# Swapped head copies, moved values and scale, split loads of x, and line loops that read and write other layouts, in an eight-stage kernel on one core

## The chip, the core and the metric

One core of a Trainium2 chip runs the whole program. The metric is the device time of one execution in microseconds. The engines are TensorE (PE; PEld is its weight load), VectorE (DVE), ScalarE (ACT), GpSimd (POOL) and SyncE (SP, which only issues transfers).

## What is computed

Eight images of 64 channels, 32x32, pass through a non-local block (attention over all 1,024 positions of an image), four recurrent passes of a nine-tap convolution (down, up, right, left), and then four token stages (window attention, spectral mixing, linear attention, experts), which the change does not touch. The first two, cut to what matters:

```python
def _L0_conv_ref(x, w_theta, w_phi, w_g, w_last):
    xf = x.reshape(B, C, H * W)
    theta = einsum('kc,bcn->bkn', w_theta, xf)          # 32 x 1024 an image
    phi, g = ...                                        # likewise
    attn = softmax(einsum('bkn,bkm->bnm', theta, phi), axis=-1)
    y = einsum('bnm,bkm->bkn', attn, g)
    return einsum('ck,bkn->bcn', w_last, y).reshape(B, C, H, W) + x

def _pass_fwd(out, w, b, axis):                         # _pass_bwd: the same from the last line back
    def step(carry, x):
        new = x + relu(conv1d(carry, w, b))
        return new, new
    ...
# forward and backward over rows (axis 2), then forward and backward over columns (axis 3)
```

## The kernel before

`setup_stage` loads x (two transfers of 1 MB, one on the queue of SyncE, one on that of ScalarE) and four small weights, zeroes some tiles on GpSimd and VectorE and writes the identity. Its block ends only when x has landed (`sp.wait_ge(x_in, 32)`).

`nonlocal_stage` is one block. Images are taken in two quads of four (q); image im of a quad has its 32 channels of theta and phi on partitions 32 im to 32 im + 31, which is also its row tile in TensorE. `project` makes theta and phi of a quad (L177), ScalarE and VectorE copy them to SBUF (L283, L312). Then `score(q, k, pair)` (L193) makes, for two images, the 128x1024 block of scores of 128 positions: two halves of 512 columns, each from the row tile of its image, into PSUM tile `ps[im]`. VectorE takes the maximum of each block (L316), ScalarE its exponential with the sum beside it (L289); the result is thrown away, only maximum and sum are kept. There are 64 such blocks of 128 rows, 16 groups of four. `score` of a pair waits until the exponentials of the same pair in the group before are done. Behind the last block come `values` (L202: g for all images, from x), the logarithm of the sums, the cut of maximum minus logarithm into three bf16 pieces (L318 to L326), `turn_shift` (L209: those pieces turned so that positions lie along the free axis) and copies of both to SBUF.

Then the attention: 32 units u (quad, half of the positions, block k). `score_t(u)` makes the transposed scores of four images with four products on four row tiles (L225) and adds the shift with four bf16 products of 3 rows (L229); ScalarE exponentiates them pair by pair (L302) through a ring of three PSUM tiles; `attend(u)` multiplies with the values (L241). TensorE's order is attend(u), score_t(u+2), and behind the first two units of each group of eight one `output` (L250) for the group before. VectorE copies the heads (L337) and adds the outputs to `m.rows` (L341).

`weights_stage` prepares weights. `conv_passes` runs 61 steps over the lines of a grid: TensorE adds the line by the identity (L385) and five shifted products (L388), VectorE adds bias, takes the maximum and so makes the new line (L405), ScalarE saves it to the grid (L419) and fetches the line two steps ahead into `added` (L414). TensorE waits for `fetch_ok` and, ahead of the shifted products, for `line_ok`. It runs first on `m.rows`, then `rows_to_cols_stage` (L449) copies everything into `m.cols`, it runs on `m.cols`, and `cols_to_tokens_stage` (L468) copies into `m.x`, where the token stages read. Both moves are three copies of 64x2048 on VectorE and one on ScalarE. GpSimd works out the spectral weights beside the vertical passes.

## Time and profile before

| | us |
|---|---|
| three timed runs | 1627.47, 1628.1, 1633.12 (median 1628.1) |
| the profiled run | 1628.84, its span 1627.1 |
| PE busy | 1440.0 (89% of the span) |
| DVE busy | 680.8 (42%) |
| ACT busy | 563.2 (35%) |
| POOL busy | 137.8 (8%) |
| mean granted TensorE clock | 0.919 |

The share of busy time is a mean over stages with different limits. A TensorE record is one pass; an fp32 product has two, with a load of weights for each. Times of the trace count from the first instruction. The clock is told as a share of 2.4 GHz, 0.5 being 1.2 GHz; for the first 23 us of this span there is no record of it, and the length of a pass tells it.

### The profile page before, as it was taken

What the parts mean: (1) busy time and instruction counts of PE and PEld (TensorE: products, weight loads), DVE (VectorE), ACT (ScalarE), POOL (GpSimd) and SP (SyncE); (2) the same over time, 40 slices, a digit from 0 to 9 for tenths busy, and PEclk for the clock granted to TensorE, in tenths of its full rate; (3) what the DMA queues carried; (4) which work ended last, traced back from release to release, by engine and by line L of the source; (5) the groups of instructions that cost most, each with busy time, mean ns of one, the idle gap of its engine ahead of it and who ended that gap; (6) DMA issues with size and microseconds to landing.
All of it is one profiled execution on the core that took longest, in us unless ns stands there. A gap on an engine that the chain in (4) does not pass through costs nothing. (4 is left out here: it accounts for less than half of the span.)

```text
span 1627.1 us, 25795 instructions
## 1 busy us (share of the span) xinstructions
PE 1440.0 (89%) x9714; PEld 977.4 (60%) x9714; DVE 680.8 (42%) x963; ACT 563.2 (35%) x913; POOL 137.8 (8%) x243
## 2 busy tenths in 40 slices
PE   4888997887887799999988999999999999958767
PEld 1335225776776699999985555555555555537544
DVE  3664013113112677777753333332333323326562
ACT  2654674223223443434343222222222212214250
POOL 5000002930000111111100000000000000003000
PEclk9555897999998999999999999999999999979977
DMA  4900000000000500000000000000000000040001
GB/s 98 104 1 1 1 1 3 0 0 0 0 0 21 186 0 0 0 0 0 0 1 1 0 0 0 0 0 0 0 0 0 0 0 0 0 100 5 1 1 52
DMA packets 34241, 23.48 MB, mean 14 GB/s; under 512 B 24621, under 2 KB 28749, under 8 KB 34205
## 3 DMA queue, kind: packets, MB, share of 16 engines
q1 hardware_dynamic: 33837, 21.92, 6.2%
q10 hardware_dynamic: 368, 1.07, 0.3%
q8 instruction: 24, 0.39, 0.1%
q14 instruction: 12, 0.10, 0.0%
HBM read 20.80 MB, written 2.18 MB: 14 GB/s over the span
## 5 line engine op out<-in xcount | busy, mean ns | idle before, releaser
L948 PE MATMUL sp_f<-hankel,sp_ut 128*128 x2304 | 420.9, 344 | 0.0
L948 PEld LDWEIGHTS sp_f<-hankel,sp_ut 128*128 128x128 f16 x2304 | 222.8, 98 | 216.7 <-issue 27.5
L987 ACT COPY sp_sums<-sp_f 64x1023 f32<-64x1023 f32 x128 | 129.0, 1008 | 427.6 <-PE sp_f L948 427.6
L1010 DVE COPY sp_sums<-sp_f 64x1024 f32<-64x1024 f32 x128 | 155.2, 1212 | 91.9 <-PE sp_f L948 91.9
L1008 DVE COPY sp_mix<-mix 128x512 f32 x64 | 27.3, 427 | 281.6 <-PE sp_f L948 281.6
L959 PE MATMUL sp_o<-sp_sums,sp_mix 128*64 128x128 f32 (+2 forms) x1024 | 123.7, 392 | 0.0
L193 PE MATMUL nl_ps<-mix 32*128 32x512 f32 x256 | 94.2, 1065 | 22.0 <-ACT nl_spent L289 22.0
L388 PE MATMUL convh<-runningh,toeplitz 128*128 128x128 f32 x610 | 85.9, 287 | 15.2 <-DVE runningh L405 15.2
L388 PE MATMUL convv<-runningv,toeplitz 128*128 128x128 f32 x610 | 85.8, 287 | 15.2 <-DVE runningv L405 15.2
L316 DVE TENSOR_REDUCE nl_max<-nl_ps 128x1 f32<-128x1024 f32 x64 | 74.0, 1218 | 43.3 <-PE nl_ps L193 43.3
L388 PEld LDWEIGHTS convh<-runningh,toeplitz 128*128 128x128 f32 x610 | 74.4, 192 | 26.7 <-DVE runningh L405 26.7
L388 PEld LDWEIGHTS convv<-runningv,toeplitz 128*128 128x128 f32 x610 | 74.2, 191 | 26.7 <-DVE runningv L405 26.7
L289 ACT ACTIVATE nl_spent<-nl_ps,nl_max 128x1024 bf16<-128x1024 f32 x64 | 71.3, 1114 | 46.7 <-DVE nl_max L316 46.7
L959 PEld LDWEIGHTS sp_o<-sp_sums,sp_mix 128*64 128x64 f32 x1024 | 63.2, 134 | 37.4 <-issue 15.6
L193 PEld LDWEIGHTS nl_ps<-mix 32*128 32x128 f32 x256 | 36.8, 310 | 78.6 <-ACT nl_spent L289 44.8
L302 ACT ACTIVATE nl_probs_t<-nl_ps 128x1024 f32<-128x1024 f32 x64 | 62.0, 1021 | 25.6 <-PE nl_ps L229 25.6
L688 PEld LDWEIGHTS s_ps<-win_x,queries 128*128 128x128 f32 x512 | 68.4, 194 | 2.6
L688 PE MATMUL s_ps<-win_x,queries 128*128 128x128 f32 x512 | 68.5, 277 | 0.0
L705 PE MATMUL z_ps<-win_heads_t,win_vo 128*128 128x128 f32 x512 | 62.6, 275 | 2.2 <-ACT win_heads_t L767 2.2
L717 PE MATMUL z_ps<-win_probs_t,win_xt 128*128 128x128 f32 x512 | 62.6, 275 | 1.4 <-ACT win_probs_t L761 0.8
L761 ACT ACTIVATE win_probs_t<-t_ps 128x512 f32<-128x512 f32 x32 | 19.1, 598 | 123.5 <-PE t_ps L699 123.5
L705 PEld LDWEIGHTS z_ps<-win_heads_t,win_vo 128*128 128x128 f32 x512 | 59.7, 192 | 2.6 <-ACT win_heads_t L767 2.6
(299 smaller groups left out, 1828.4 us busy)
## 6 DMA issues: line engine op xcount, KB each, us to landing
hankel<-phi_rows SPq DMA_DIRECT2D x32, 256.0 KB, 6.0
ex_w<-in_L_ffn_weight SPq DMA_DIRECT2D x1, 2080.0 KB
m_plus<-in_L_ffn_M_phi_plus SPq DMA_DIRECT2D x2, 1024.0 KB, 14.0
m_minus<-in_L_ffn_M_phi_minus SPq DMA_DIRECT2D x2, 1024.0 KB, 16.3
out<-x SPq DMA_DIRECT2D x8, 256.0 KB, 3.3
x<-in_x SPq DMA_DIRECT2D x1, 1024.0 KB, 8.5
x<-in_x ACTq DMA_DIRECT2D x1, 1024.0 KB, 12.4
ar<-in_L_ffn_M_u SPq DMA_DIRECT2D x2, 192.0 KB, 3.1
```

The source lines that it names most:

```text
L193: mm = nc.tensor.matmul(ps[im][:, c * BANK:(c + 1) * BANK], theta[q][rows_of(im), k * P:(k + 1) * P], phi[q][rows_of(im), c * BANK:(c + 1) ...
L289: nc.scalar.activation(spent[im][:, :], ps[im][:, :], ACT.Exp, bias=nmax[:, q, k, im:im + 1], accum_out=rsum[:, q, k, im:im + 1]).then_inc ...
L302: nc.scalar.activation(probs_t[u % 2][:, 2 * pair:2 * pair + 2, :].rearrange("p a n -> p (a n)"), ps[j % 3][:, :], ACT.Exp).then_inc(p_ok, 1)
L316: nc.vector.tensor_reduce(nmax[:, q, k, im:im + 1], ps[im][:, :], axis=AX.X, op=ALU.max, negate=True).then_inc(mx_ok, 1)
L388: mm = nc.tensor.matmul(conv[odd][:, :, :], m.toeplitz[:, wn, s, :], running[1 - odd][:, :, s:s + PAIRS], start=False, stop=(s == SHIFTS - 1))
L688: mm = nc.tensor.matmul(s_ps[:, hg, w, :], queries[:, w, 4 * hg:4 * hg + 4, :].rearrange("p h n -> p (h n)"), m.win_x[:, w, :, :].rearrang ...
L705: mm = nc.tensor.matmul(o_ps, m.win_vo[:, h, :], heads_t[:, h // 4, :, (h % 4) * WINDOW:(h % 4 + 1) * WINDOW], start=(h == 0), stop=(h == ...
L717: mm = nc.tensor.matmul(z_ps[:, hg, w, :], xt[odd][:, w, :], probs_t[:, hg, w, :], start=True, stop=True)
L948: mm = nc.tensor.matmul(f_ps[b][:, lo:(half + 1) * BANK], ut[:, hu, b, i, :, :].rearrange("p a c -> p (a c)"), m.hankel[:, hf, ds(j * 2 + ...
L959: mm = nc.tensor.matmul(out_of(lo, cnt, par), mixk[n][:, SCALES - 1 - seg, par, :], sums[n][:, :, lo + par:lo + cnt:2], start=False, stop= ...
L987: nc.scalar.copy(sums[n][HALF[1], b, 1:T], f_ps[b][HALF[1], 0:T - 1]).then_inc(f_act, 1)
L1010: nc.vector.tensor_copy(sums[n][HALF[0], b, :], f_ps[b][HALF[0], :]).then_inc(f_dve, 1)
```

## The change

Setup: x comes in halves of two image pairs each, behind the small weights, on the same two queues, with a semaphore for each half (`m.x_in[q]`), and the block no longer waits for them. TensorE makes 24 products of the identity with itself there. The zeroing of `rows` moves into the non-local block, that of the `lin_` tiles to VectorE, that of `cols` goes.

Non-local: theta (whole) and phi (its second half of the columns) get copies with the two halves of the partitions swapped (`theta_b`, `phi_b`). Of a block of scores the first 512 columns come from the image's own row tile, the other 512 from the tile two further on, so that a pair of images fills all four. The four PSUM tiles are two pairs used in turn. `values` stands behind the first pair of scores. The shift is the negated maximum alone, with no logarithm, cut and turned by quads, the first quad's in the middle of the scores, the second's turned at units 2 and 6 of the attention. The reciprocals of the sums are spread over 32 channels, turned (`turn_scale`, once in each group of eight units) and multiplied onto the heads. In `score_t` the shifts of the first pair come ahead of the scores and those of the second behind them.

Lines: `conv_passes` is given an object that fetches and stores. The horizontal passes read their lines out of `m.rows` on the way forward (two copies of 64x128 a line), keep them in `m.cols`, fetch them from there on the way back and store each line straight into `m.x` (four copies of 64x64). Line 0 and the last line are brought to `m.x` by GpSimd. The two moving stages are gone.

```diff
@@ setup_stage
+    WARM = 24
...
+                for q in range(2):
+                    eng.dma_start(m.x[HALF[p], 2 * q:2 * q + 2, :], ins["x"][4 * q + p:4 * q + 4:2].rearrange("g c h w -> c g (h w)")).then_inc(m.x_in[q], 16)
-                sp.wait_ge(x_in, 32)
+            @block.tensor
+            def _(pe):
+                pe.wait_ge(ident_ok, 1)
+                for n in range(WARM):
+                    mm = nc.tensor.matmul(warm_ps[:, :], m.ident[:, :], m.ident[:, :], start=True, stop=True)
+                mm.then_inc(warm, 1)
@@ nonlocal_stage, GpSimd
+                pool.wait_ge(q_act, 3)
+                pool.wait_ge(q_dve, 5)
+                for g in range(2):
+                    nc.gpsimd.tensor_copy(theta_b[HALF[1 - g], 1, :], theta[1][HALF[g], :]).then_inc(q_pool, 1)
...
+                    nc.gpsimd.tensor_copy(phi_b[HALF[1 - g], 1, :], phi[1][HALF[g], BANK:T]).then_inc(q_pool, 1)
...
+                nc.gpsimd.memset(m.rows[:, :, :, :], 0.0).then_inc(zeroed, 1)
+        TURN_AT = {2: 0, 6: 1}
+        SCALE_AT = 4
@@ TensorE
+                def score(s):
+                    q, k, pair = s // (2 * NB), s // 2 % NB, s % 2
...
+                    elif s == 1:
+                        pe.wait_ge(ex_ok, 2)
+                    elif s == 2:
+                        pe.wait_ge(v_c, 2)
                     else:
+                        pe.wait_ge(ex_ok, 2 * (s - 1))
+                    if s == PAIRED // 2:
+                        pe.wait_ge(q_pool, 4)
+                    for j, im in enumerate((2 * pair, 2 * pair + 1)):
+                        nc.tensor.matmul(slots(s)[j][:, 0:BANK], theta[q][rows_of(im), k * P:(k + 1) * P], phi[q][rows_of(im), 0:BANK], start=True, stop=True)
+                    for j, im in enumerate((2 * pair, 2 * pair + 1)):
+                        far = rows_of((im + 2) % QUAD)
+                        nc.tensor.matmul(slots(s)[j][:, BANK:T], theta_b[far, q, k * P:(k + 1) * P], phi_b[far, q, :], start=True, stop=True).then_inc(s_ok, 1)
...
+                    shifted(0, True)
...
+                        pe.wait_ge(p_ok, 2 * u - 1)
                     for im in range(QUAD):
+                        mm = nc.tensor.matmul(out[im], phi[q][rows_of(im), k * P:(k + 1) * P], theta[q][rows_of(im), c * BANK:(c + 1) * BANK],
+                                              start=(im >= 2), stop=(im < 2))
+                        if im == 1:
                             mm.then_inc(t_ok, 1)
+                    shifted(1, False).then_inc(t_ok, 1)
...
+                def turn_scale(w):
+                    q, c = w // NH, w % NH
+                    pe.wait_ge(wide_ok, q + 1)
+                    use_out()
+                    for k in range(NB // NH):
+                        mm = nc.tensor.matmul(o_ps[:, k * P:(k + 1) * P], wide[:, q, c * NB // NH + k, :, :].rearrange("p i c -> p (i c)"), m.ident[:, :],
+                                              start=True, stop=True)
+                    mm.then_inc(o_ok, 1)
...
+                score(0)
+                values()
+                for s in range(1, PAIRED):
+                    score(s)
+                pe.wait_ge(cut_ok, 1)
+                pe.wait_ge(ex_ok, ROWS - 2)
+                turn_shift(0, 0, ps[3][:, 0:BANK])
+                turn_shift(0, 1, ps[3][:, BANK:T]).then_inc(turn_ok, 1)
...
+                    if u in TURN_AT:
+                        pe.wait_ge(cut_ok, 2)
+                        use_out()
+                        turn_shift(1, TURN_AT[u], o_ps).then_inc(o_ok, 1)
+                    if u % NB == SCALE_AT:
+                        turn_scale(u // NB)
@@ ScalarE
-                nc.scalar.activation(rest[:, :, :, :], rsum[:, :, :, :], ACT.Ln).then_inc(ln_ok, 1)
@@ VectorE
+                    if n == ROWS // NQ + 1:
+                        dve.wait_ge(mx_ok, ROWS // NQ)
+                        cut(0)
...
+                nc.vector.tensor_copy(shift_t[0][:, :], ps[3][:, :]).then_inc(turn_c, 1)
+                dve.wait_ge(mx_ok, ROWS)
+                cut(1)
...
+                    nc.vector.tensor_tensor(heads[w % 2][:, :], y_ps, scale_t[w % 2][:, :], ALU.mult).then_inc(y_c, 1)
@@ lines
+class ColumnLines:
...
+    def column(self, pair, par, hp):
+        return self.rows[HALF[par], hp::2, :, ds(PADP + pair, 1)].rearrange("c r b a -> c b (r a)")
+
+    def token(self, pair, par, hp, p):
+        x = self.x[HALF[p], :, :].rearrange("c g (r a w) -> c g r a w", a=2, w=W)
+        return x[:, :, :, hp, ds(pair * 2 + par, 1)].rearrange("c g r w -> c g (r w)")
+
+    def fetch(self, copy, dst, pair, par):
+        for hp in range(2):
+            last = copy(dst[HALF[hp], :, :], self.column(pair, par, hp))
+        return last
...
+    def store(self, copy, line, pair, par):
+        for hp in range(2):
+            for p in range(2):
+                last = copy(self.token(pair, par, hp, p), line[HALF[hp], p::2, :])
+        return last
@@ hybrid_program
-            conv_passes(nc, m, m.rows, 0, "v", lambda block: spectral_mixing(nc, m, block, mixing_step))
-            rows_to_cols_stage(nc, m)
-            conv_passes(nc, m, m.cols, 2, "h")
-            cols_to_tokens_stage(nc, m)
+            vertical_passes(nc, m, mixing_step)
+            horizontal_passes(nc, m)
```

## Rows read from the trace of the kernel before

**Rows 1.** Windows: stretch, its length, each engine's busy time (records), clock, DMA.
```profile
27.95:146.66 118.71, 94.19 (x259) 36.83 (x257) 75.18 (x65) 72.56 (x127) 1.06 (x1) 0.52 0.34 42
146.66:165.96 19.30, 18.13 (x92) 16.09 (x92) 3.90 (x7) 5.92 (x7) 0.00 (x0) 0.50 0.00 1
165.96:258.34 92.38, 85.12 (x692) 22.73 (x692) 8.31 (x12) 62.01 (x64) 0.00 (x1) 0.96 0.00 1
...
394.85:400.92 6.07, 0.00 (x0) 0.00 (x0) 5.68 (x3) 3.71 (x1) 0.00 (x0) 0.81 0.00 0
...
517.58:524.32 6.74, 0.00 (x0) 0.00 (x0) 5.65 (x3) 3.68 (x1) 0.00 (x0) 0.54 0.00 0
```
**Rows 2.** Timeline of one group of scores, of 16: start, length, instruction.
```profile
93.30 6.05 PE L193 MATMUL nl_ps<-mix 32*128 32x512 f32 x16 [1.41 <-ACT nl_spent L289]
...
97.11 4.62 DVE L316 TENSOR_REDUCE nl_max<-nl_ps 128x1 f32<-128x1024 f32 x4 [2.84 <-PE nl_ps L193]
...
98.37 1.11 ACT L289 ACTIVATE nl_spent<-nl_ps,nl_max 128x1024 bf16<-128x1024 f32 x1 [2.86 <-DVE nl_max L316]
...
100.75 0.50 PEld L193 LDWEIGHTS nl_ps<-mix 32*128 32x128 f32 x4 [2.98 <-ACT nl_spent L289]
```
**Rows 3.** Groups by line: the projections up to 22.9 us, and from 23.7 us.
```profile
L177 PE MATMUL nl_ps<-x,nl_proj 128*64 128x512 f32 x10 | 4.5, 1068 | 3.8 <-ACT nl_last L280 3.8
...
L177 PE MATMUL nl_ps<-x,nl_proj 128*64 128x512 f32 x22 | 4.9, 596 | 0.0
```
**Rows 4.** Timeline of the setup and the start of the non-local stage.
```profile
1.39 0.29 POOL L78 TENSOR_SCALAR_AFFINE_SELECT ident<-ident 128x128 f32<-128x128 f32 x1 [0.23 <-POOL average L76]
...
13.96 0.26 POOL L150 MEMSET nl_proj<- 128x192 f32 x1 [7.03 <-POOLq L55]
...
16.48 0.54 DVE L309 COPY nl_proj<-nl_ps 64x96 f32<-64x96 f32 x2 [9.01 <-POOL nl_pieces L153]
...
18.78 9.24 PE L177 MATMUL nl_ps<-x,nl_proj 128*64 128x512 f32 x32 [3.81 <-ACT nl_last L280]
```
**Rows 5.** Timeline by engine between the last scores and the first probability.
```profile
146.66 13.92 PE L202 MATMUL nl_ps<-nl_proj,x 128*128 128x64 f32 x64 [2.55 <-ACT nl_spent L289]
...
161.46 1.23 DVE L328 CAST nl_shift_t<-nl_ps 128x1024 bf16<-128x1024 f32 x1 [10.45 <-PE nl_ps L209]
...
165.96 1.94 ACT L302 ACTIVATE nl_probs_t<-nl_ps 128x1024 f32<-128x1024 f32 x2 [1.34 <-PE nl_ps L229]
```
**Rows 6.** Timeline of the attention: a unit with an output, and a plain one.
```profile
214.73 1.13 PE L250 MATMUL nl_ps<-nl_heads,nl_last 128*64 128x256 f32 x8
...
215.78 1.07 PE L241 MATMUL nl_ps<-nl_probs_t,mix 128*32 128x512 f32 x8
...
216.78 1.14 PE L225 MATMUL nl_ps<-mix 32*128 32x512 f32 x8
...
218.07 1.13 PE L250 MATMUL nl_ps<-nl_heads,nl_last 128*64 128x256 f32 x8
...
227.50 1.14 PE L225 MATMUL nl_ps<-mix 32*128 32x512 f32 x8
...
229.96 1.14 PE L225 MATMUL nl_ps<-mix 32*128 32x512 f32 x8
```
**Rows 7.** Timeline of one conv step, of 61; the window of the horizontal loop's start.
```profile
295.38 1.39 PE L388 MATMUL convv<-runningv,toeplitz 128*128 128x128 f32 x10 [0.29 <-DVE runningv L405]
295.46 0.30 ACT L419 COPY rows<-runningv 128x128 f32 x1 [1.40 <-DVE runningv L405]
295.67 0.30 ACT L414 COPY addedv<-rows 128x128 f32 x1
...
296.61 0.39 PE L385 MATMUL convv<-addedv,ident 128*128 128x128 f32 x2
...
297.21 1.20 PEld L388 LDWEIGHTS convv<-runningv,toeplitz 128*128 128x128 f32 x10 [0.41 <-DVE runningv L405]
...
400.92:405.50 4.58, 4.21 (x18) 3.92 (x19) 0.96 (x4) 1.01 (x4) 0.00 (x0) 0.51 0.00 0
```

More of the change, by code:

```diff
@@ L198, in values @@
-                def values(half):
-                    pe.wait_ge(ex_ok, ROWS - 1 + half)
-                    for g in (2 * half, 2 * half + 1):
-                        for k in range(NB):
-                            mm = nc.tensor.matmul(ps[2 + half][:, (g % 2) * BANK + k * C:(g % 2) * BANK + (k + 1) * C], m.x[:, g, k * P:(k + 1) * P],
-                                                  proj[:, 2, :, :].rearrange("p a k -> p (a k)"), start=True, stop=True)
-                    mm.then_inc(v_ok, 1)
@@ L411, in _, with fetch, step @@
                 act.sem_inc(saved, 1)
-                def fetch(line, odd):
-                    nc.scalar.copy(added[odd][:, :, :], at(line)).then_inc(fetch_ok, 1)
-                def step(n, odd, line, ahead=None):
+                def fetch(pair, odd, back):
+                    (lines.refetch if back else lines.fetch)(nc.scalar.copy, added[odd][:, :, :], pair, odd).then_inc(fetch_ok, 1)
+                def step(n, odd, pair, back):
                     act.wait_ge(line_ok, n + 1)
-                    nc.scalar.copy(at(line), running[odd][:, :, PADP:PADP + PAIRS]).then_inc(saved, 1)
-                    if isinstance(ahead, int) and ahead >= 2 * TOP - 3:
-                        act.wait_ge(saved, n + 1)
-                    if ahead is not None:
-                        fetch(ahead, odd)
+                    (lines.store if back else lines.keep)(nc.scalar.copy, inner(running[odd]), pair, odd).then_inc(saved, 1)
@@ L463, in cols_to_tokens_stage @@
[L463 to L479 removed]
+                    step(n, n % 2, (2 * FWD - n) // 2, True)
@@ new lines, in vertical_passes, with horizontal_passes, ends, _ @@
+def vertical_passes(nc, m, mixing_step):
+    conv_passes(nc, m, RowLines(m), 0, "v", lambda block, saved, n: spectral_mixing(nc, m, block, mixing_step))
+def horizontal_passes(nc, m):
+    lines = ColumnLines(m)
+    def ends(block, saved, n):
+        @block.gpsimd
+        def _(pool):
+            for hp in range(2):
+                for p in range(2):
+                    src = m.rows[HALF[0], hp::2, p::2, PADP:PADP + 1].rearrange("c r g a -> c g (r a)")
+                    nc.gpsimd.tensor_copy(lines.token(0, 0, hp, p), src)
+            pool.wait_ge(saved, n)
+            lines.store(nc.gpsimd.tensor_copy, lines.at(W // 2 - 1, 1), W // 2 - 1, 1)
+    conv_passes(nc, m, lines, 2, "h", ends)
```

355 lines of the change are left out of this document (202 added, 153 removed).

## The prediction

> **What bounds the kernel now.** I first cut the span into stretches by the table of windows [rows 1]: 118.7 us of scores, 19.3 us between them and the first probability, 92.4 us of attention, and two stretches of 6.07 and 6.74 us in which TensorE does nothing. The change touches these, the 28 us ahead of them and the two line loops around the moves; the 1,100 us behind 524.3 us it leaves alone. Then I read who waits for whom in each.
>
> The scores go in groups of four rows of blocks, 16 groups, 7.45 us each (LDWEIGHTS at 93.30 and 100.75) [rows 2]. No engine is full: the four reductions take 4.62 us, the exponentials about the same. It is a ring: TensorE writes the first pair's two PSUM tiles (93.30 to 97.11, 3.81 us), VectorE reduces one (1.26 us), ScalarE exponentiates two (98.37 to 100.75, 2.38 us), and only then may TensorE write again. The 3.81 us are four passes of 0.86 us one after another, two products side by side. 0.86 us is the length of a 512-column pass at 1.2 GHz: in the projections such a pair took 0.86 us (10 records in 4.5 us) and then 0.43 us (22 records in 4.9 us) once the clock had risen to 2.4 GHz [rows 3]; the granted clock of the score stretch is 0.52 [rows 1].
>
> The attention is bound by TensorE's own sequence and a ring of about the same length: 2.46 us for a plain unit (227.50 to 229.96), 3.34 us for a unit with an output (214.73 to 218.07), of which output 1.05, attend 1.00, scores and shifts 1.29 [rows 6].
>
> A conv step is a ring of TensorE and VectorE, with ScalarE beside: it saves a line at 295.46, fetches at 295.67 and is done at 295.97; the product that needs the fetched line starts at 296.61, the next step's weight loads at 297.21, 1.83 us behind the last ones [rows 7].
>
> **Part 1, start.** The wait for x at the end of the setup goes; in its place stand 24 products of 128x128 fp32 from 1.68 us on, when the identity is written [rows 4]. A pass of 128 columns is 0.11 us at 2.4 GHz (10 records in 1.39 us, less the tail of the last [rows 7]), so 0.22 at 1.2, and a product two passes. All cold 10.6 us, all warm 5.3; I take 11 cold and 13 warm, 7.8 us, so the stage ends at 9.5 us, bound by these products, and the next begins at about 10.1 instead of 13.96 [rows 4]. From there to the turned weights in SBUF is GpSimd's four memsets and two copies, 13.96 to 17.02: 3.1 us, unchanged. The first projection no longer waits for the ScalarE copies, so it starts at 13.3 instead of 18.78. x had landed by 13.96 with both megabytes; its first half, now two small loads later, should be in by 12. I expect TensorE, idle for most of 9.5 to 13.3, to be back at 1.2 GHz, and the projections to take their 9.24 us again [rows 4]: they end at 22.5 instead of 28.0. If the clock holds they take 32 x 0.215 = 6.9 us, 2.3 less.
>
> **Part 2, values moved.** Their 64 records took 13.9 us at 1.2 GHz, between scores and attention [rows 5]. Now they stand behind the first score pair, right behind the projections, where the clock is up: 64 x 0.11 = 7.0 us, all on the path, since every later score is queued behind them. The end for a clock that falls first is 13.9. They wait for phi of the second quad, a copy of 1.2 us like the one at 161.46 (together about 1.35 us behind the last projection, the first score pair and VectorE's swapped copies lying in it). 22.5 + 1.35 + 7.0 + 1.15 for the next pair: VectorE's regular work starts at 32.0. GpSimd's swapped copies for the second quad, its memset and its placing of x run beside this; they are due at the seventeenth pair and at the first addition.
>
> **Part 3, scores.** Both halves of a row's columns go to four row tiles at once: two passes instead of four, so 3.81 - 2 x 0.86 = 2.1 us at 1.2 GHz and about 1.17 at 2.4 (the attention's eight records on four tiles take 1.14 [rows 6]). The four PSUM tiles are now two pairs with a ring each. The ring is 2.1 + 1.26 + 2.38 = 5.75 us for four rows (4.8 warm); the engines' floor is VectorE's 4.62 [rows 2]. Which clock? Before, at 1.2 GHz, the engine was busy 94 of 119 us on half its rows and never rose [rows 1]. Now it would be busy a third less of the time on all rows, about the same work in a little less time. I take 1.2 GHz. 30 pairs x 2.88 = 86.3 us from 32.0, plus 0.7 for the first quad's cut, which now stands in VectorE's queue between two reductions: the last pair's reductions start at 119.0.
>
> **Part 4, from scores to attention.** Gone are the logarithm, two table loads and one cut from the path. What is late next is VectorE: last reductions until 121.4, the shift's copy 1.2, then shifts and scores of the first unit, 2.3 us cold. First probability at 125.0 instead of 165.96 [rows 5]: 41.0 us earlier.
>
> **Part 5, attention.** It lasted 92.1 us from 165.96 (the window's 92.38 less the end of the block) [rows 1]. Added to TensorE's sequence: four turns of the sums (eight passes of 0.11 and a drain, nearest row the output's 1.05): 4.2 us; two half turns of the second shift in bf16, 0.45 each: 0.9. The multiplication takes the place of a copy of the same shape. The shifts are split: those of the first pair ahead of the scores, those of the second behind. A bf16 pass of 512 columns is half an fp32 pass of 0.43, 0.21 us. If tiles run free of one another the unit stays at 2.29 us of TensorE work (1.00 + 1.29) and the ring shrinks to 1.02 (an exponential) + 0.06 + 1.17 = 2.25: 0.17 less for 23 plain units, -3.9. If products start strictly in the order written, the second pair's scores stand behind the first pair's, which wait for their shifts: 2.29 + 0.21 = 2.50, +1 in plain units and +0.21 in the six with an output, +1.3. So between +1.2 and +7.4 in all. In the rows no product is seen overtaking another, so I take +7.4.
> The Trainium skill ("TensorE: Matmul & The Clock Gate", Part 3, What overlaps and what doesn't) says that products start and end strictly in program order whatever their tiles. By it the sum is +7.4; with free tiles it would be +1.2.
>
> **Part 6, lines.** Both moving stages go: 6.07 us, and of the second stretch the same 6.07, while 0.67 of it is the next stage's start [rows 1]. Added: the first fetch is four half copies instead of two (+0.4), the last save four quarter copies (+0.6). In the loop ScalarE has a save and two half fetches forward, four quarter stores and a fetch backward. A 128-element copy follows the next after 0.21 us [rows 7]; the strided move took 3.71 us for 2,048 elements [rows 1], 1.8 ns each, so 64 cost 0.09 + 0.12 = 0.2. Backward: 4 x 0.2 + 0.3 = 1.1 us from 295.46, to 296.56, against 296.61, and a wait would hurt only 0.39 us ahead of 297.21, from 296.82 on [rows 7]. Hidden, if a store costs under 0.26; at 0.3 it would cost 30 x 0.15 = 4.5 us. Line 0 and the last column go over GpSimd, beside. TensorE's pause shrinks from 7 to 2 us at one place and from 8 to 2.5 at the other: the loop's start took 4.58 us for 18 records at clock 0.51 [rows 7], some 1.6 more than warm. I take 1.3 for it and 0.5 for the norm (0 to 3).
>
> **Sum.** -41.0 + 7.4 - 12.1 + 1.0 - 1.8 = -46.5 us against a span of 1627.1, in a run of 1628.84, which is 0.7 above the median: 1628.1 - 46.5 = 1581.6.
>
> **Rivals.**
> A, free tiles in the attention: 6.2 less, 1575.4. The rows don't exclude it.
> B, the scores run at 2.4 GHz, and emptying PSUM decides: 30 pairs x 2.31 to 2.4 us is 14 to 17 us less, a warm start of the attention 2 more: 1564. For it: the values before it are warm and all row tiles are used; against: pauses of over 1 us in every 2.4. The Trainium skill ("TensorEngine Tiling (Array Packing)", PSUM Bottleneck) warns that after a fourfold speed-up the copy out of PSUM may be the limit. By that rule the group takes 4.62 us and not 5.75, which is this rival.
> C, values at 1.2 GHz: +6.9 us, 1588.5. For it: a pause before them; against: the projections just before are full work.
> D, the four products don't run side by side (it doesn't do what it says): the ring stays 7.45, +26 us, 1608. Against: the attention's scores, four tiles, eight records in 1.14 us [rows 6].
> E, slower than before: ScalarE's quarter copies with columns 256 bytes apart take over the backward loop. A store of 0.26 us is where it starts; at 0.66 a step takes 1.55 us more, 30 steps 46.5 us, the whole gain; above 0.66 the kernel is slower, at 0.8 it takes 1581.6 + 30 x 2.14 = 1646. Against: 1.8 ns an element in the strided move.
>
> **Chances.** Forecast 45% (1574 to 1589 by its own bounds), A 27, B 10, C 9, other prices of the conv loop and the start, 1585 to 1600, 4, D 2, E 3. The range takes all but the outer ends of B, D and E: 1564 to 1592. A measurement of this kernel tells about 0.5% (8 us) from no change. Faster by more: 95%; within 0.5%: 2%; slower: 3%.
>
> **What would show it.** First projection at 13.3 us; first warm pass of the values at 24 with 0.11 us between; groups of four rows 5.75 us apart (4.8: B; 7.45: D); first probability at 125; plain units 2.50 (2.29: A), units with an output 3.55; no pause over 2.5 us between the loops; conv steps still 1.83 to 1.90 us, backward too. The forecast is wrong if the score stretch runs at another clock or if the backward steps are longer.

## The result and the profile after

The changed kernel takes 1584.1 us (median of four runs, 1579.14 to 1585.12) against 1628.3 us for the kernel before (four runs beside it, 1627.47 to 1633.12): ratio 0.972, 95% interval 0.969 to 0.974. The forecast was 1581.6 us, its range 1564 to 1592. The profiled run took 1585.12 us, its span is 1583.3 us, 43.8 us less than before; the mean granted clock is 0.929 (before 0.919).

The windows of the changed kernel, cut where its stages change (stretch, length, busy time of PE, PEld, DVE, ACT, POOL with records, clock, DMA); the lines of before that they answer to are [rows 1]. The clock has no record before 6.7 us, so the 1.00 of the first line doesn't hold for all of it; the passes themselves tell: 22 of 0.21 us up to 6.6 us, which is 1.2 GHz, then 26 of 0.11 us:

```profile
0.00:9.98 9.98, 7.97 (x48) 7.78 (x48) 2.71 (x8) 0.00 (x0) 1.14 (x9) 1.00 0.71 147
9.98:21.81 11.83, 9.35 (x45) 2.99 (x45) 3.27 (x6) 5.17 (x8) 2.41 (x4) 0.86 0.65 145
21.81:30.55 8.74, 8.39 (x74) 7.53 (x72) 3.49 (x3) 3.35 (x5) 7.01 (x5) 1.00 0.27 53
30.55:118.56 88.01, 60.59 (x249) 15.16 (x249) 73.58 (x66) 69.92 (x120) 8.67 (x5) 0.56 0.45 52
118.56:123.33 4.77, 3.37 (x22) 1.82 (x22) 4.57 (x11) 2.33 (x4) 0.00 (x0) 0.50 0.00 0
123.33:220.19 96.86, 92.51 (x734) 30.49 (x730) 13.14 (x19) 62.07 (x64) 0.00 (x1) 0.92 0.00 1
220.19:240.20 20.01, 15.08 (x122) 13.04 (x122) 11.43 (x25) 10.70 (x14) 4.90 (x21) 0.50 0.04 6
357.35:478.20 120.85, 106.33 (x732) 91.14 (x732) 22.40 (x65) 78.54 (x243) 2.23 (x8) 0.98 0.00 0
478.20:1583.30 1105.10, 1019.64 (x7044) 709.39 (x7044) 522.66 (x712) 338.12 (x449) 54.23 (x151) 0.96 0.05 14
```

The first probability stands at 123.33 us where it stood at 165.96: 42.6 us are won up to there. The attention gives back 4.5 us (96.86 against 92.38). Between the vertical and the horizontal passes 6.1 us are gone; horizontal passes and second move together give 2.6 us (from 123.4 to 120.85). The vertical passes take 0.6 us more, and the token stages, whose code is the same, 2.3 us more. -42.6 + 4.5 - 6.1 - 2.6 + 0.6 + 2.3 = -43.9 us, the 43.8 us of the spans but for rounding.

The start, timeline of TensorE (start, length, instruction, idle before it and what ended that); before, the projections began at 18.78 [rows 4] and the values took 13.92 us [rows 5]:

```profile
1.73 7.97 PE L79 MATMUL warm_ps<-ident 128*128 128x128 f32 x48 [1.73 <-POOL ident L87]
...
13.10 1.60 PE L205 MATMUL nl_ps<-x,nl_proj 128*64 128x512 f32 x4 [2.44 <-DVE nl_proj L372]
...
23.30 7.33 PE L215 MATMUL nl_ps<-nl_proj,x 128*128 128x64 f32 x64 [0.35 <-DVE mix L381]
```

One turn of the score ring, timeline; it answers to [rows 2]:

```profile
88.49 2.36 DVE L407 TENSOR_REDUCE nl_max<-nl_ps 128x1 f32<-128x1024 f32 x2 [0.22 <-PE nl_ps L236]
...
89.56 1.22 PE L233 MATMUL nl_ps<-mix 32*128 32x512 f32 x2 [1.12 <-ACT nl_spent L358]
...
89.57 1.22 PE L236 MATMUL nl_ps<-nl_phi_b,nl_theta_b 32*128 32x512 f32 x2
...
89.75 1.11 ACT L358 ACTIVATE nl_spent<-nl_ps,nl_max 128x1024 bf16<-128x1024 f32 x1 [0.24 <-DVE nl_max L407]
...
90.58 1.06 PE L233 MATMUL nl_ps<-mix 32*128 32x512 f32 x2
...
90.88 1.11 ACT L358 ACTIVATE nl_spent<-nl_ps,nl_max 128x1024 bf16<-128x1024 f32 x1
91.70 2.36 DVE L407 TENSOR_REDUCE nl_max<-nl_ps 128x1 f32<-128x1024 f32 x2 [0.86 <-PE nl_ps L236]
...
92.14 0.29 PEld L233 LDWEIGHTS nl_ps<-mix 32*128 32x128 f32 x2 [2.06 <-ACT nl_spent L358]
...
94.28 1.23 DVE L407 TENSOR_REDUCE nl_max<-nl_ps 128x1 f32<-128x1024 f32 x1 [0.22 <-PE nl_ps L236]
```

The fp32 products of a pair take two passes one after another, 89.56 to 91.70 (2.14 us), where before there were four: the two halves of a row start 0.01 us apart. VectorE starts a pair at 88.49 and at 94.28: 5.79 us for four rows where it was 7.45. It still idles (0.22 and 0.86 us), because a pair's first product waits for both exponentials of that PSUM pair: the first ends 1.1 us before the second, and its tile stands empty. This turn ran at 1.2 GHz, like most of the stretch.

### The profile page after: what moved, and what is told of

Read it like the earlier page. It is cut to its first block and busy times, and to the rows that moved or that the text cites. A ratio compares the mean times of both kernels' runs of the same rounds, so it can differ in the third digit from the quotient of the medians.

```text
span 1583.3 us, 26273 instructions
## 1 busy us (share of the span) xinstructions
PE 1423.7 (90%) x9794; PEld 968.1 (61%) x9794; DVE 679.3 (43%) x977; ACT 601.3 (38%) x1029; POOL 138.5 (9%) x251
## 5 line engine op out<-in xcount | busy, mean ns | idle before, releaser
L1113 PEld LDWEIGHTS sp_o<-sp_sums,sp_mix 128*64 128x64 f32 x1024 | 63.1, 134 | 37.4 <-issue 15.5
L233 PE MATMUL nl_ps<-mix 32*128 32x512 f32 x128 | 61.3, 1052 | 26.2 <-ACT nl_spent L358 26.0
L365 ACT ACTIVATE cols<-nl_ps 128x1024 f32<-128x1024 f32 x64 | 62.1, 1022 | 29.6 <-PE nl_ps L269 29.6
L522 DVE SCALAR_TENSOR_TENSOR runningh<-convh,conv_bias,addedh 128x128 f32<-128x128 f32 x61 | 21.5, 352 | 96.1 <-PE convh L505 96.1
L948 DVE TENSOR_REDUCE win_max<-s_ps 128x16 f32<-128x1024 f32 x32 | 39.2, 1225 | 53.3 <-PE s_ps L842 53.3
```

What stands on the lines that cost most here:

```text
L233: nc.tensor.matmul(slots(s)[j][:, 0:BANK], theta[q][rows_of(im), k * P:(k + 1) * P], phi[q][rows_of(im), 0:BANK], start=True, stop=True)
L365: nc.scalar.activation(probs_t[u % 2][:, 2 * pair:2 * pair + 2, :].rearrange("p a n -> p (a n)"), ring[j % 3][:, :], ACT.Exp).then_inc(p_o ...
L1113: mm = nc.tensor.matmul(out_of(lo, cnt, par), mixk[n][:, SCALES - 1 - seg, par, :], sums[n][:, :, lo + par:lo + cnt:2], start=False, stop= ...
```

## Experiments

All edits are to the changed kernel, except where another is named. Where one time is given, the kernel was run once; it is compared with 1584.1 us, and its trace with the trace of the changed kernel. Four runs of the changed kernel lie 6 us apart, and beside own_tiles, values_back, stores_twice and one_pause the kernel before took 1631.4 us in the median, 3 us more than beside the changed kernel. So a single time says little below some 5 us, and the readings rest on the stages in the traces.

**Release by rows.** The products of a row wait for the exponential of that row's own PSUM tile, and a row's two halves are issued together.

```diff
-                    elif s == 1:
-                        pe.wait_ge(ex_ok, 2)
...
-                    else:
-                        pe.wait_ge(ex_ok, 2 * (s - 1))
...
                     for j, im in enumerate((2 * pair, 2 * pair + 1)):
+                        if s == 1 or s >= 3:
+                            pe.wait_ge(ex_ok, max(2 * (s - 2), 0) + j + 1)
                         nc.tensor.matmul(slots(s)[j][:, 0:BANK], ...)
-                    for j, im in enumerate((2 * pair, 2 * pair + 1)):
                         far = rows_of((im + 2) % QUAD)
                         nc.tensor.matmul(slots(s)[j][:, BANK:T], ...)
```

> The changed kernel with one thing moved: a row's two score products wait for the exponential of the row that last used their PSUM tile, not for both rows of the pair, and are issued row by row. Theory (the scores are bound by the ring of a pair: TensorE 2.1 us, a reduction 1.26, two exponentials and the way back 2.38, together 5.75 for four rows): a row's own ring is 2.1 + 1.26 + 1.13 + 0.15 = 4.65 for four rows, so VectorE's four reductions of 4.62 us become the bound, even at 1.2 GHz. The last pair's reductions then start some 17 us earlier (at 100 to 101 us instead of 117.4) and the run takes about 1567 us. Rival 1 (TensorE's 1.2 GHz is the bound as such): the group stays at 5.75 us and the time at 1584. Rival 2 (products of the next row wait until those of the row before have ended): the ring grows to 2.1 + 2.1 + 1.26 + 1.13 and the group to 6 us or more, 1588 or slower.

Measured: 1564.8 us (1563.16 to 1565.64, four runs), ratio 0.961 (0.958 to 0.963). The windows of its scores, and of the part of them that ran at 1.2 GHz:

```profile
31.80:101.19 69.39, 65.98 (x236) 20.74 (x232) 69.17 (x66) 68.14 (x120) 6.38 (x4) 0.85 0.54 63
35.60:45.80 10.20, 10.20 (x36) 4.26 (x36) 10.16 (x10) 10.12 (x19) 2.70 (x2) 0.50 0.92 119
```

VectorE is busy 69.17 of 69.39 us: it is the bound, 4.6 us for four rows. The granted clock of the stretch rose from 0.56 to 0.85, but the gain doesn't hang on it: from 35.6 to 45.8 us the clock was 0.50, and VectorE was busy 10.16 of 10.20 us. So at 1.2 GHz it was the wait for two exponentials, and not the length of the products, that held the ring at 5.8 us. The third and fourth units of the attention started 3.31 and 2.29 us behind the ones before instead of 4.55 and 3.26: both kernels began the attention at 1.2 GHz, but here the clock rose 5.0 us behind the first probability (at 110.7 us) and there 9.7 us behind it.

**The tiles of the own image again.** The second half of a row's columns from the row tile of its own image, once with release by pairs (own_tiles), once with release by rows (own_by_row).

```diff
-                        far = rows_of((im + 2) % QUAD)
-                        nc.tensor.matmul(slots(s)[j][:, BANK:T], theta_b[far, q, k * P:(k + 1) * P], phi_b[far, q, :], start=True, stop=True).then_inc(s_ok, 1)
+                        nc.tensor.matmul(slots(s)[j][:, BANK:T], theta[q][rows_of(im), k * P:(k + 1) * P], phi[q][rows_of(im), BANK:T], start=True, stop=True).then_inc(s_ok, 1)
```

> The changed kernel with one part undone: the second half of a row's columns comes again from the row tile of the row's own image (theta, phi), so that a pair of rows is four passes one after another; the swapped copies are still made and not read. My theory: the ring of four rows is 7.45 us as in the kernel before instead of 5.78, 15 groups, +25 us: 1609 us. Rival (the ring was shorter in the changed kernel because its four PSUM tiles are used as two pairs in turn, not because of the tiles): 1584 to 1590 us.

> Release row by row, and both halves of a row's columns again from the row tile of its own image (the swapped copies are still made, but not read), so that a row is four passes one after another. Theory 1 (what the swapped copies bought was only a shorter ring, and with release by rows the ring of each slot has room): at 2.4 GHz a slot's ring is 1.75 products + 1.2 reduction + 1.35 exponential = 4.3 us against VectorE's 4.6 us for four rows, so 1565 us as with the swapped copies. Theory 2 (the copies are needed because the clock is low in this stretch): at 1.2 GHz the ring is 3.45 + 2.55 = 6.0 us for four rows, 16 x 1.4 = 22 us more, 1587 us. The granted clock of the score stretch tells which.

Measured: own_tiles 1609.7 us (one run), own_by_row 1590.8 us (1589.96 to 1595.16, four runs), ratio 0.978 (0.976 to 0.980). In own_tiles the last reduction comes 110.92 us behind the fourth, 60 rows: 7.39 us for four rows, as before the change, against 85.62 us and 5.71. So the tiles gave the change's shorter ring; the turns of the PSUM tiles gave nothing. For own_by_row theory 2 held, 6.29 us for four rows. The window of its scores:

```profile
34.10:128.50 94.40, 93.25 (x236) 56.37 (x235) 72.82 (x66) 71.11 (x121) 5.13 (x3) 0.52 0.40 46
```

TensorE is busy 93.25 of 94.40 us, and its clock is 0.52 all the same. The busy time counts any row tile at work; each of them still waits. One PSUM tile's turn lasts 6.33 us (its products start at 71.76 and again at 78.09 us): 3.8 us for the row's four passes one after another, 1.26 for the reduction and 1.25 for the exponential. So the ring of a single tile sets the end, and the products at 1.2 GHz are its longest part. Over the 60 rows behind the fourth the swapped copies are worth 25.3 us with release by pairs (110.92 against 85.62) and 25.0 us with release by rows (94.38 against 69.39).

**Values behind the scores again.**

```diff
-                score(0)
-                values()
-                for s in range(1, PAIRED):
+                for s in range(PAIRED):
                     score(s)
-                pe.wait_ge(cut_ok, 1)
                 pe.wait_ge(ex_ok, ROWS - 2)
+                values()
+                pe.wait_ge(cut_ok, 1)
+                pe.wait_ge(v_c, 2)
```

(The two copies of the values move to the same place on ScalarE and VectorE, and the third pair of scores no longer waits for them but for theta and phi of the second quad.)

> The changed kernel with one part undone: the products of the values stand behind the last pair of scores again and not behind the first. My theory (their price is their clock): before the steady scores 8.5 us less (7.3 for the products, 1.2 for the copy), behind them 13.9 at 1.2 GHz and 1.2 for the copy, of which 1.2 to 3 us lie beside the last reductions and exponentials; +4 to +6 us, 1588 to 1590 us, first probability 4 to 6 us later than 123.3. Rival (the products are full work and bring the clock up wherever they stand): 7.3 us there too, and the attention starts at full clock: 1578 to 1583 us.

Measured: 1591.4 us, first probability at 135.19, 11.9 us later. Timeline of TensorE, and the window of the values:

```profile
115.17 13.91 PE L215 MATMUL nl_ps<-nl_proj,x 128*128 128x64 f32 x64 [1.13 <-ACT nl_spent L356]
```

```profile
115.00:129.40 14.40, 13.91 (x64) 13.72 (x64) 1.72 (x3) 3.47 (x7) 0.00 (x0) 0.50 0.00 0
```

The price was right (13.9 us at 1.2 GHz, no rise of the clock in full work), the gain at the front was not: steady work began 3.3 us earlier, not 8.5. The second pair uses the PSUM tiles of the first and waits for its exponentials until 26.41; in the changed kernel that wait lies beside the values. So the move is worth more at the first probability, 11.9 us, than the difference of two lengths. Of these the end shows 6.2: the attention's first to last probability took 1.1 us less, the stretch from there to the first line of the vertical passes 1.4, and the token stages 3.0, all of the same code as in the changed kernel.

**No warm products.** The TensorE block of the setup is left out.

> The changed kernel without the 24 warm products. Theory (they bind the end of the setup, at 9.7 us, and their warmth is lost before the projections): the non-local stage begins at 4 to 4.5 us instead of 9.98, the turned weights are there at 7.7, and the first projection starts when the first half of x has landed, 9.6 us instead of 13.1. The projections still begin at 1.2 GHz, the rest is 3.5 us earlier: 1580.5. Rival (the warm products bring the clock up for the projections or the values): without them the projections take 9.2 us or more instead of 8.7 and the values 13.9 us instead of 7.3, which takes back all of it: 1584 to 1588.

Measured: 1581.5 us; first projection at 9.42, released by x's arrival:

```profile
9.42 2.83 PE L199 MATMUL nl_ps<-x,nl_proj 128*64 128x512 f32 x6 [4.21 <-DMA x<-in_x]
```

First probability at 119.57 instead of 123.33. From the first to the last start of a projection it is 8.22 us, with the 24 products 8.19. They held up the next stage by 3.7 us, and nothing of it came back up to the first probability.

**Shifts behind the scores for all four images.**

```diff
-                    shifted(0, True)
...
-                                              start=(im >= 2), stop=(im < 2))
-                        if im == 1:
-                            mm.then_inc(t_ok, 1)
+                                              start=True, stop=False)
+                    shifted(0, False).then_inc(t_ok, 1)
                     shifted(1, False).then_inc(t_ok, 1)
```

> The changed kernel with all four shifts of an attention unit behind its scores, as before the change. Theory (row tiles run free of one another, so a shift ahead of one pair's scores hides under the other pair's, and the first probability of a unit may start before the last shifts): undoing it brings the ring back to 1.02 + 0.06 + 1.38, plain units back from 2.29-2.37 to 2.46 us, some 0.1 x 24 = 2 to 3 us longer attention (96.9 to about 99.5 us). Rival (products start strictly in the order written, and the split only costs): plain units fall to 2.29 us by TensorE's work or stay, the attention gets shorter by up to 5 us.

Measured: 1585.2 us. Plain units are 2.55 us apart (163.93 - 161.38 by the exponentials below) instead of 2.29 and 2.37 by turns; first to last probability 90.22 us instead of 88.30. In the kernel before they were 2.46 us apart with all shifts behind [rows 6]; what the other 0.09 us are, no run shows.

```profile
158.83 1.94 ACT L363 ACTIVATE cols<-nl_ps 128x1024 f32<-128x1024 f32 x2 [1.41 <-PE nl_ps L251]
161.38 1.94 ACT L363 ACTIVATE cols<-nl_ps 128x1024 f32<-128x1024 f32 x2 [0.61 <-PE nl_ps L251]
163.93 1.94 ACT L363 ACTIVATE cols<-nl_ps 128x1024 f32<-128x1024 f32 x2 [0.61 <-PE nl_ps L251]
```

The 1.9 us between the two sums hide a difference of the clock: here it rose 6.2 us behind the first probability and there 9.7, so the first three starts of a unit took 9.72 us against 11.01. In the 28 starts behind them, all at 2.4 GHz, it is 79.58 against 76.37 us: the split is worth 3.2 us.

**Fetch ahead of the stores** in the backward loop.

```diff
-                        step(k * 2 + odd, odd, k * (-1) + (FWD - odd), True)
+                        act.wait_ge(line_ok, k * 2 + odd + 1)
                         fetch(k * (-1) + (FWD - 1 - odd), odd, True)
+                        step(k * 2 + odd, odd, k * (-1) + (FWD - odd), True)
```

> The changed kernel with ScalarE's order on the way back of the horizontal passes turned round: it fetches the line two steps ahead first and then makes the four quarter stores of the new line. Theory (the backward step is 1.946 instead of 1.865 us because the fetch stands behind four stores of 0.31 us and TensorE waits for it): the fetch ends 0.3 us behind the new line instead of 1.55, the step falls back to 1.865 us, 30 steps give 2.4 us. Rival (the stores slow the step by themselves, through SBUF writes 256 bytes apart or VectorE's wait for the saved line): the step stays at 1.95 us. Time 1581 against 1584 by the theory, which a single time can't tell; the step in the trace does.

Measured: 1580.0 us. 30 backward steps took 56.00 us, as many forward ones 56.01; in the changed kernel 58.34 and 56.00. Timeline of ScalarE and VectorE in two backward steps, with the identity product in the first; first the changed kernel, then with the fetch first:

```profile
431.32 1.23 ACT L612 COPY x<-runningh 64x64 f32 x4 [0.54 <-DVE runningh L522]
432.57 0.30 ACT L604 COPY addedh<-cols 128x128 f32 x1
432.65 0.35 DVE L522 SCALAR_TENSOR_TENSOR runningh<-convh,conv_bias,addedh 128x128 f32<-128x128 f32 x1 [1.48 <-PE convh L505]
...
433.00 0.48 PE L502 MATMUL convh<-addedh,ident 128*128 128x128 f32 x2 [0.39 <-DVE runningh L522]
...
434.71 0.35 DVE L522 SCALAR_TENSOR_TENSOR runningh<-convh,conv_bias,addedh 128x128 f32<-128x128 f32 x1 [1.72 <-PE convh L505]
```

```profile
434.16 0.30 ACT L605 COPY addedh<-cols 128x128 f32 x1 [0.41 <-DVE runningh L522]
434.37 1.23 ACT L613 COPY x<-runningh 64x64 f32 x4
...
435.50 0.35 DVE L522 SCALAR_TENSOR_TENSOR runningh<-convh,conv_bias,addedh 128x128 f32<-128x128 f32 x1 [1.55 <-PE convh L505]
...
437.33 0.35 DVE L522 SCALAR_TENSOR_TENSOR runningh<-convh,conv_bias,addedh 128x128 f32<-128x128 f32 x1 [1.48 <-PE convh L505]
```

In the changed kernel the four stores take 1.23 us, the fetch ends at 432.87, and the identity product starts at 433.00 instead of running ahead of the line at 432.65: steps of 1.83 and 2.07 us by turns. With the fetch first 1.83 and 1.90.

**Stores twice.** Eight quarter copies a line in the backward loop, four of them into a spare tile of the same layout.

```diff
-    def store(self, copy, line, pair, par):
-        for hp in range(2):
-            for p in range(2):
-                last = copy(self.token(pair, par, hp, p), line[HALF[hp], p::2, :])
+    def store(self, copy, line, pair, par, into=(None,)):
+        for x in into:
+            for hp in range(2):
+                for p in range(2):
+                    last = copy(self.token(pair, par, hp, p, x), line[HALF[hp], p::2, :])
```

> The changed kernel with the four quarter copies of the backward horizontal loop issued twice, the first four into a spare tile of the same layout: eight copies of 0.31 us stand for four of 0.62. The law of my rival E, every store above 0.26 us lengthens a step by four times the excess: 1.87 + 4 x 0.36 = 3.3 us a step, 30 steps, +40 us against the changed kernel's 1.95: 1624 us. Rival, ScalarE's own work is the bound and nothing more: 8 x 0.31 + 0.30 for the fetch + 0.2 = 3.0 us a step, +31 us, 1615 us. Second rival, half of the excess because a fetch serves the step after the next: 2.6 us a step, +20 us, 1604 us.

Measured: 1608.0 us; the last 30 steps in 79.64 us against 58.34. The 28 of them that have the stores in the loop take 2.55 and 2.84 us by turns, 2.7 a step. Timeline of ScalarE in one step:

```profile
434.54 0.30 ACT L607 COPY addedh<-cols 128x128 f32 x1
434.75 1.23 ACT L616 COPY spare_xh<-runningh 64x64 f32 x4
...
436.00 1.23 ACT L616 COPY x<-runningh 64x64 f32 x4
...
437.25 0.30 ACT L607 COPY addedh<-cols 128x128 f32 x1
```

No idle time stands before any of them: ScalarE's own row of copies is the bound, 8 x 0.31 + 0.21 = 2.7 us from fetch to fetch (my sum of 3.0 counted 0.3 us too much around it). The second rival's 2.6 us lies near too, but it has ScalarE waiting, which it doesn't. Rival E's law was too steep by half: the steps cost 21.3 us more than with four stores, not 40. By an estimate from this row of copies, 4 x s + 0.21 us a step, a store would have to cost 0.8 us, not 0.66, before the loop ate the whole gain of 46.5 us (4 x 0.8 + 0.21 = 3.4, 1.55 more than 1.87).

**Three edits together**: release by rows, fetch first, and warm products where TensorE waits anyway (5 products in the setup, 11 behind the transposes of the small weights). The same without any warm products is lean.

```diff
-    WARM = 24
+    WARM = 5
...
                 mm.then_inc(lt_ok, 1)
+                for n in range(11):
+                    nc.tensor.matmul(ps[1][:, 0:P], m.ident[:, :], m.ident[:, :], start=True, stop=True)
                 pe.wait_ge(wt_c, 2)
```

> Three edits together: products of a row wait only for their own slot's last exponential; the backward line loop fetches ahead of its stores; of the 24 warm products 5 stay in the setup and 11 move behind the transposes of the small weights, beside the ScalarE and GpSimd copies that the first projection waits for. My theory (the three terms are independent: 1564.8 us with the first alone, -2.4 for the fetch, and at the start -3.65 for what the 24 products held up and up to -1.3 more because the projections now start at full clock, a pair 0.43 us apart from the first one): 1557.5 us. First projection at 9.5 us, last projection starting 6.8 us behind the first instead of 8.2. Rival, the projections wait for x and not for TensorE: they start again late or pause, 1559 to 1560. Rival, VectorE's 4.6 us per four rows is not the end and the earlier start only shifts the clock: back to 1562 or more.

> The same as the kernel with the three edits, but all 24 warm products left out and none moved. My theory, that warm products pay only where they stand beside a wait directly ahead of the projections: 1558.8 us, first projection at 9.4 us, last projection starting 8.2 us behind it. If the difference to the kernel with the moved products is 0 or below, they are worth nothing here.

Measured: three edits 1556.0 us (1553.95 to 1558.85, four runs), ratio 0.956 (0.954 to 0.959); lean 1559.5 us (1558.11 to 1559.67, four runs), ratio 0.959 (0.957 to 0.960). Timeline of TensorE with the three edits:

```profile
1.74 2.50 PE L79 MATMUL warm_ps<-ident 128*128 128x128 f32 x10 [1.74 <-POOL ident L87]
...
5.45 5.00 PE L197 MATMUL nl_ps<-ident 128*128 128x128 f32 x22
10.38 1.08 PE L207 MATMUL nl_ps<-x,nl_proj 128*64 128x512 f32 x4
```

All 22 passes ran at 1.2 GHz (5.00 us, 0.227 us each) and ended 0.9 us after x was there (9.53 in lean), and the projections right behind them ran at 2.4 GHz from the first one on (the granted clock rose at 10.3 us), 6.53 us from first to last start against 8.43 in lean. The last reduction is 0.85 us earlier than in lean. The medians are 3.5 us apart, but the intervals of the two ratios overlap and the two traces differ by 0.2 us in span, so more than 1 us for the moved products isn't shown.

**Pauses filled.** On top of the three edits, three products of 128x128 fp32 behind the last line step of both line blocks and three more ahead of the first horizontal step (filled); the same between the vertical and the horizontal passes alone (one_pause, whose diff this is).

```diff
                     mm.then_inc(conv_ok, 1)
+                def filler():
+                    for n in range(3):
+                        nc.tensor.matmul(conv[0][:, :, :], m.ident[:, :], m.ident[:, :], start=True, stop=True)
+                if tag == "h":
+                    filler()
                 steps(pe, step)
+                if tag == "v":
+                    filler()
```

> The kernel with the three edits, and in both line blocks three products of 128x128 fp32 behind the last line step (beside the last VectorE and ScalarE work), and in the horizontal block three more ahead of the first step (beside the first fetches). Theory (the clock falls behind these pauses because TensorE did nothing in them): full clock in the first 12 us of the horizontal passes and of the first layer norm, 1 to 2 us less than the kernel with the three edits. Rival (the clock falls for another reason, or these stretches are bound by other engines): within 0.5 us of it, or up to 0.5 us slower, as the three products end after the wait that they stand beside.

> The kernel with the three edits, and products to fill the pause between the vertical and the horizontal passes alone: three of 128x128 fp32 behind the last vertical step, three ahead of the first horizontal one. In the trace of the kernel that filled three pauses the first horizontal line was ready 3.59 us behind the last vertical one instead of 4.89. Theory, that 1.3 us is a gain: the same 3.6 us here, and 1.3 us less than the 1556.0 us of the three edits, 1554.7. Rival, the time is given back in the clock of later stretches: 1556 to 1558 us.

Measured: filled 1558.0 us (1556.52 to 1558.92, four runs), ratio 0.958 (0.956 to 0.959); one_pause 1558.6 us (1554.7 to 1559.4, five runs), ratio 0.955 (0.953 to 0.956), with runs of before between 1629.09 and 1635.07 us beside it, 4 us higher in the median than beside the others. Timeline of TensorE and VectorE of one_pause:

```profile
330.85 0.35 DVE L529 SCALAR_TENSOR_TENSOR runningv<-convv,conv_bias,addedv 128x128 f32<-128x128 f32 x1 [1.48 <-PE convv L504]
...
331.84 0.91 PE L510 MATMUL convh<-ident 128*128 128x128 f32 x6 [0.36 <-PEq L494]
...
333.11 1.28 PE L504 MATMUL convh<-runningh,toeplitz 128*128 128x128 f32 x10
...
334.43 0.35 DVE L529 SCALAR_TENSOR_TENSOR runningh<-convh,conv_bias,addedh 128x128 f32<-128x128 f32 x1 [1.54 <-PE convh L504]
```

From the last vertical to the first horizontal line it is 3.58 us (334.43 - 330.85), 3.59 in filled, and 4.90 with the three edits alone; the window of 334.4 to 345 us has clock 1.00 instead of 0.84 (filled against the three edits). So a filled pause gives 1.3 us in its place; the whole doesn't show it. In the traces the attention of filled took 0.8 us more and its token stages 1.7 more. The kernels with the three edits lie at 0.955 to 0.959 of the time before; which of them is the best, these runs don't tell.

## Why the prediction was right, and where it was not

**Start.** Right: first projection at 13.10 (forecast 13.3), their end at 21.9 (22.5); 11 of the 24 products ran at 1.2 GHz, as the prediction took it. The clock was lost, if a little later than forecast: TensorE idled 2.44 us, the first projection still began at 2.4 GHz (13.10 to 13.62 us, then 0.86 us for each pair), and the granted clock was 0.50 from 13.5 to 16.9 us. The prediction took the 24 products for a bound of the stage, 9.5 us, and didn't say that without them the time would be 3.7 us less; no_warm showed it.

**Values.** 7.33 us (7.0), VectorE's steady work from 31.8 us on (32.0). Rival C is out. At the first probability the move is worth 11.9 us, more than 13.9 - 7.3, by values_back.

**Scores.** The ring of 5.75 us was right to 0.05 at 1.2 GHz, and the clock was low for most of the stretch (0.56). The last pair's reductions came at 117.4 us (119.0), since the clock was up until 37.4 us and again from 85.2 to 88.6 us. There rival B's ring shows, timeline of VectorE:

```profile
83.65 4.62 DVE L407 TENSOR_REDUCE nl_max<-nl_ps 128x1 f32<-128x1024 f32 x4 [0.94 <-PE nl_ps L236]
```

The next pair stands at 88.49: 4.84 us for four rows, where rival B has 4.8. So B had the ring right and the clock wrong. Its time, 1564, is what by_row reached, in another way: in these traces the full clock and the release by rows each bring four rows under 4.9 us. Rival D is out by own_tiles, and by the starts 0.01 us apart.

**First probability.** 123.3 us (125.0); the difference is the 1.6 us of the scores.

**Attention.** The step that failed is the assumption that products start in the order written; by it plain units would be 2.50 us. They were 2.29 (161.43 - 159.14) and 2.37 us (163.80 - 161.43). Timeline of the changed kernel, ScalarE and TensorE, for [rows 6]:

```profile
159.14 1.94 ACT L365 ACTIVATE cols<-nl_ps 128x1024 f32<-128x1024 f32 x2 [1.41 <-PE nl_ps L269]
...
161.43 1.94 ACT L365 ACTIVATE cols<-nl_ps 128x1024 f32<-128x1024 f32 x2 [0.35 <-PE nl_ps L269]
...
162.50 0.39 PE L251 MATMUL nl_ps<-nl_shift_t,nl_ones 3*128 3x512 bf16 x2
...
162.52 1.23 PE L269 MATMUL nl_ps<-mix 32*128 32x512 f32 x8
...
163.48 0.38 PE L251 MATMUL nl_ps<-nl_shift_t,nl_ones 3*128 3x512 bf16 x2
163.79 0.86 PEld L306 LDWEIGHTS nl_ps<-ident,nl_theta_b 128*128 128x128 f32 x7 [0.64 <-issue]
...
163.80 1.02 ACT L365 ACTIVATE cols<-nl_ps 128x1024 f32<-128x1024 f32 x1 [0.43 <-PE nl_ps L269]
```

The first scores start 0.02 us behind the shifts, not 0.21. The group of eight passes is four starts: two passes at 162.52, two at 162.73, two at 163.05, two at 163.16; the one that signals the second image's scores, written ahead of all of the third and fourth image, is the last of them. So the third and fourth image's products, on free row tiles, overtook. This is rival A's mechanism. The Trainium skill ("TensorE: Matmul & The Clock Gate", Part 3) has products strictly in program order; these rows don't agree, and the measurement decides.

By rival A the attention would be +1.2 us; it was +4.5, short of the +7.4 of the forecast. What the sum left out is mostly clock. It was 0.50 up to 133.0 us, 9.7 us behind the first probability (before, 7.3 us), and the first three starts of a unit took 11.01 us where they took 10.20. It was 0.50 again from 214.9 us on, so that the last two outputs took 1.73 and 1.98 us instead of about 1.1; from the last exponential on it is 1.5 us more than before. The 28 starts between, at 2.4 GHz, took 2.2 us more than before, 1.0 more than rival A has for the whole. Two errors of opposite sign, then: -6.2 us for the order, +3.3 us for the rest, of which the clock has 2.3.

**Lines.** Both moves are gone, 6.07 us each, as forecast. A store costs 0.31 us from start to start (forecast 0.2), because copies of 64 strided elements don't overlap: 0.30 us long, four in 1.23 us. This is the second step that failed: the stores weren't hidden. The backward steps were 1.95 us and not 1.87, which the prediction had named as a sign of being wrong, 2.3 us in 30. Its law for a store above 0.26 us gives 6 at 0.31; where the threshold lies, no run shows. TensorE's pauses shrank to 1.97 and 2.75 us, but the clock fell in both all the same (358.3 to 361.7 and 477.7 to 481.1 us at 0.50), so of the forecast 1.8 us of clock little came: the first 30 steps took 56.00 us against 56.37. With products in the pause the first horizontal line came 1.3 us earlier. In all the lines gave 8.7 us (6.1 + 2.6) where the sum has 12.4 up to the norm.

**The rest.** The vertical passes took 0.6 us more and the token stages 2.3. In the traces of this study their span, from the last horizontal line on, lies between 1104.7 (values_back) and 1110.4 us (stores_twice) with the same code. The sum for the stages up to there, -46.1 us against a forecast of -46.5, is better than its terms, and that is luck: 1.6 us more were won up to the first probability and 2.9 us less lost in the attention than forecast, the lines gave 3.7 us less, the norm's 0.5 didn't come, and the vertical passes took 0.6 more. By its mechanism the prediction was right up to the attention, and wrong in the order of the products there and in the stores; the first was named as rival A, at 27%.

## What to carry to other kernels

When a ring of buffers is shortened by faster products, look at what each wait asks for: a wait for a pair, where one tile is needed, cost here 1.2 us in every 5.8 at 1.2 GHz. Taking it away while the swapped copies were read also raised the granted clock of the stretch, to 0.63 in one trace and 0.85 in another; the length was the same, some 70 us, in both. Before an idle engine is given filler work, ask who starts behind it: 24 products cost 3.7 us. With 16, of which 11 stood directly ahead of the projections, the first projection came 0.85 us later than without any and the last reduction 0.85 us earlier. A strided copy on an engine with little to spare goes behind what others wait for, not ahead of it.

## What the runs showed of the hardware

- Products on row tiles that were free started ahead of earlier ones whose tiles were busy: scores of the third and fourth image at 162.52 us, of the first and second at 162.73, against the order written.
- Stretches with the same amount of products: TensorE busy 93.25 of 94.40 us, each row's passes on one row tile, granted clock 0.52 (own_by_row); busy 65.98 of 69.39 us, passes of a row on two tiles at once, granted clock 0.85 (by_row). But with the same score code as by_row the three edits had 0.63 (28.6 to 98.7 us, busy 67.87 of 70.13), so the tiles alone don't set the clock; what does stays open. Values on all rows stayed at 0.50 for 13.9 us of full work in values_back, and ran at 1.00 in the changed kernel, right behind the first scores.
- Copies of 64x64 elements with strided columns on ScalarE follow one another after 0.31 us; a contiguous copy of 128x128 is followed after 0.21 us, though both are 0.30 us long. The strided fetch of 128 elements takes 0.42 us (four in 1.69).
- Stages of one and the same code, some 1,107 us long, differed by 5.7 us between traces; why, no run shows. Gains of 1 to 2 us are to be read in the stage itself, and with the granted clock of both kernels beside them: the split of the shifts showed 1.9 us in the sum and 3.2 us at like clock.
